# A graph attention layer on one core: the conversion of the adjacency matrix moved from GpSimd to VectorE

## The chip, the cores and the metric

The kernel runs on one core of a Trainium2 chip. The metric is the device time of one execution in microseconds (us). The core has five engines with a queue of instructions each: TensorE (PE in the profile, its weight loads as PEld), VectorE (DVE), ScalarE (ACT), GpSimd (POOL) and SyncE (SP). SP and POOL also issue DMA transfers here, and all transfers share 16 DMA engines.

## What is computed

The inputs are `x` (4096 x 256), a 0/1 matrix `adj` (4096 x 4096, float32, about 0.4% ones) and weights for 8 heads of key size 64.

```python
h = maximum(layernorm(x), 0)
adj = maximum(adj, eye)
q, k, v = h @ Wq, h @ Wk, h @ Wv                # per head
scores = q @ k.T * 64 ** -0.5
scores = scores + 0.01 * eye - 1e16 * (1 - adj)
att = softmax(scores)
return x + sum over heads of (att @ v) @ Wo
```

So every score gets a bias: 0 where `adj` is one or on the diagonal, a huge negative number elsewhere.

## The kernel before, in words

The 8 heads are worked on in two groups of 4 (`group_programs`, g = 0 and 1). A group first makes keys and values for all 4096 nodes (`keys_values`), then runs over 16 row blocks i of 256 rows (two tiles q = 0, 1 of 128 rows) and in each over its heads h = 0 to 3. One pair (i, h) is a step, 64 steps in a group. The order of every engine's work is written out by hand (`step` in each engine's program), and semaphores tie the engines together.

In step (i, h) TensorE transposes the probabilities of head h (`transposes`), multiplies them by the values (`values`, `values_late`), and between these computes the scores of the next head (`scores`, L449). The scores come in eight slots j of 128 x 1024, j = 0 to 3 for q = 0 and j = 4 to 7 for q = 1, into two PSUM buffers `psS`, so that the scores of slot j wait for the mask of slot j - 2. VectorE's `mask` (L702) adds the bias `B` to the slot, writes it to `S` and takes the row maximum. Per step VectorE runs masks 2 and 3 of the next head, `sum_halves` (L735, L740), masks 4 and 5, the denominators and sums of heads, masks 6 and 7, the transpose of half of the probabilities in 32 x 32 blocks for q = 0 (`transpose_late`, L723), masks 0 and 1 of the head after, and the transpose for q = 1. The blocks so transposed are put in their places by 32 DMA transfers per step, 64 KB each: 16 from SP (`move_late`, L248) and 16 from POOL (L307). The masks 4 to 7 write where these blocks are read from: masks 4 and 5 wait for the two halves of the moves of q = 0, masks 6 and 7 for those of q = 1. TensorE's last part of a step (`values_late`, L486) waits for all of them.

`B` (128 x 2 x 4096, bf16) holds the bias of one row block and serves all heads of it. In the first group POOL fills it: it loads eight slots of `adj` per row block with a cast to bf16 (`load_adj`, L287, 512 KB read and 256 KB written each), each as soon as the last head's mask has used the slot; it converts each slot in place (`convert`, L293: subtract 1, multiply by 8e16); and in the slot that holds the row block's own diagonal (`own_slot`, which moves from 0 to 3 over the row blocks) it multiplies 128 x 128 elements by `notI` (L298), which clears the bias on the diagonal. The loads and most converts stand in POOL's step h = 2, between and behind the moves of that step; the converts of slots (1, 2) and (1, 3) follow the moves of step h = 3. The masks of a row block's head 0 wait for `bias_ready`: masks 0 and 1 stand in VectorE's step h = 2, masks 2 to 7 in step h = 3. SP stores the finished bias in DRAM (`keep_bias`, in step h = 0), and the second group only loads it back, from SP's queue. Row block 0 is loaded and converted while keys and values are made.

The lines in question:

```python
B = sb("B", [P, QT, N], BF16)
mask: if h == 0 and norm: dve.wait_ge(bias_ready, i * SLOTS + (j + 1))
```

`norm` is true in the first group alone.

## Time and profile before

| | |
|---|---|
| three runs, us | 2713.36, 2710.54, 2719.93 (median 2713.36) |
| the profiled execution, us | 2709.6 |
| its span in the profile, us | 2708.1 |
| granted TensorE clock over the span | 0.994 of full speed |
| busy, share of the span | PE 97%, PEld 70%, DVE 83%, ACT 68%, POOL 47% |
| chain that ended last, by engine | PE 38%, SP's queue 3%, DVE 2%, DMA 2% |
| the first group's row blocks 0 to 14 | 118.8 to 1320.2 us |
| the second group's | 1473.1 to 2637.7 us |

The profile is one execution recorded by the hardware. Busy time is the share in which an engine had an instruction in work; an average hides what a single stretch is limited by. So stretches of the trace are looked at one by one, each with the times of its instructions and, in square brackets, the idle time ahead of an instruction and what ended it. A step is measured here from the first L486 matmul of one step to that of the next; the stretch that ends with the L486 matmuls of step (i, 2) is called step h = 2, and so on.

### The profile page before, as it was taken

The numbers are of one execution on the slowest core, as the hardware profiler recorded it, in microseconds if no ns is written. First come the engines' busy times: TensorE is split into PE (matmuls) and PEld (weight loads), VectorE is DVE, ScalarE is ACT, GpSimd is POOL, SyncE is SP. The second block draws the span as 40 slices with busy tenths as digits, with TensorE's granted clock in tenths as the row PEclk, the third lists the DMA queues.
The fourth block names the chain that finished last, engine by engine and source line by source line (L and its number), as shares of the span: only waits on it lengthen the run. The fifth ranks groups of instructions, "written<-read, shape, count | busy, mean of one in ns | idle before, by whom it ended". The sixth has DMA issues, their size and how long they took to land. (4 is left out here: it accounts for less than half of the span.)

```text
span 2708.1 us, 58752 instructions
## 1 busy us (share of the span) xinstructions
PE 2630.7 (97%) x17344; PEld 1901.9 (70%) x17344; DVE 2253.6 (83%) x3833; ACT 1850.8 (68%) x3041; POOL 1280.6 (47%) x2418
## 2 busy tenths in 40 slices
PE   7899999999999999999998999999999999999997
PEld 5666777767777776766766777777777777777775
DVE  6788888888888888888847888888888888888885
ACT  3576777767767676776745777777777777777774
POOL 2356655566565556655512444444444444343433
PEclk9999999999999999999999999999999999999999
DMA  6367766677776677776652566656565656555654
GB/s 163 111 143 177 184 163 175 165 168 167 173 190 170 164 177 166 171 171 169 167 142 76 146 158 151 158 142 145 138 151 145 164 146 162 133 146 138 157 144 106
DMA packets 263358, 418.51 MB, mean 155 GB/s; under 512 B 98944, under 2 KB 119936, under 8 KB 259200
## 3 DMA queue, kind: packets, MB, share of 16 engines
q1 hardware_dynamic: 172032, 228.88, 33.0%
q0 software_dynamic: 89088, 184.69, 29.7%
q10 hardware_dynamic: 2176, 4.19, 0.4%
q8 instruction: 28, 0.46, 0.1%
q14 instruction: 34, 0.28, 0.0%
HBM read 136.31 MB, written 46.27 MB: 67 GB/s over the span
## 5 line engine op out<-in xcount | busy, mean ns | idle before, releaser
L307 POOL DMA_DIRECT2D S<-S x2048 | 1007.8, 500 | 1137.1 <-DVE S L723 1089.6
L702 DVE CUSTOM_DVE_ANT_0 S<-psS,B 128x1024 f32<-128x1024 f32 x1024 | 1228.4, 1218 | 268.3 <-PE psS L449 155.1
L589 ACT ACTIVATE S<-S,negm 128x1024 f32<-128x1024 f32 (+1 forms) x768 | 1095.8, 1428 | 88.8 <-DVE negm L709 88.3
L596 ACT ACTIVATE PT<-psT 128x512 f32<-128x512 f32 x1024 | 595.0, 596 | 267.5 <-PE psT L462 248.5
L449 PE MATMUL psS<-K,QH 128*128 128x512 f32 x2048 | 729.2, 437 | 35.7 <-DVE mx L702 31.5
L449 PE MATMUL psS<-K,QL 128*128 128x512 f32 x2048 | 642.5, 395 | 0.0
L462 PEld LDWEIGHTS psT<-ident,S 128*128 128x128 f32 x4096 | 481.2, 140 | 192.0 <-issue 73.5
L462 PE MATMUL psT<-ident,S 128*128 128x128 f32 x4096 | 608.0, 276 | 7.8 <-ACT S L589 4.9
L723 DVE STREAM_TRANSPOSE S<-S 128x2048 f32<-128x2048 f32 x256 | 590.2, 2306 | 27.6 <-PE psO L486 23.7
L472 PE MATMUL psO<-PT,V 128*64 128x256 f32 x4096 | 492.1, 382 | 0.0
L486 PE MATMUL psO<-S,V 128*64 128x256 f32 x4096 | 470.3, 382 | 2.0 <-DMA S<-S 2.0
L449 PEld LDWEIGHTS psS<-K,QL 128*128 128x128 f32 x2048 | 385.3, 188 | 87.4
L486 PEld LDWEIGHTS psO<-S,V 128*64 128x64 f32 x4096 | 283.6, 137 | 176.5 <-issue 48.0
L472 PEld LDWEIGHTS psO<-PT,V 128*64 128x64 f32 x4096 | 283.4, 137 | 175.0 <-ACT PT L596 23.7
L449 PEld LDWEIGHTS psS<-K,QH 128*128 128x128 f32 x2048 | 313.6, 191 | 82.0 <-DVE mx L702 69.6
L623 ACT ACTIVATE Oodd<-psO 64x256 f32<-64x256 f32 x128 | 48.9, 382 | 400.7 <-PE psO L472 400.7
L293 POOL TENSOR_SCALAR B<-B 128x1024 bf16<-128x1024 bf16 x128 | 133.4, 1052 | 59.6 <-DMA B<-in_adj 58.4
L589 ACT ACTIVATION_READ_ACCUMULATOR S<-S,negm 128x1 f32 x768 | 146.0, 190 | 0.0
L685 DVE TENSOR_TENSOR QL<-psP,QH 64x256 fp32r<-64x256 f32 x248 | 104.4, 421 | 3.6
L708 DVE TENSOR_TENSOR S<-S,diag 128x128 f32 (+1 forms) x256 | 75.2, 294 | 30.9 <-DVE mx L702 23.3
L580 ACT ACTIVATE QH<-psP 64x256 fp32r<-64x256 f32 x248 | 93.1, 375 | 2.2
L702 DVE DVE_READ_ACCUMULATOR2_ANT mx<- 128x1 f32 x1024 | 84.9, 83 | 0.0
(51 smaller groups left out, 967.9 us busy)
## 6 DMA issues: line engine op xcount, KB each, us to landing
S<-S SPq DMA_DIRECT2D x2048, 64.0 KB, 3.1
S<-S POOLq DMA_DIRECT2D x2048, 64.0 KB, 2.9
B<-in_adj POOLq DMA_DIRECT2D x128, 256.0 KB, 7.2
bias_scratch<-B SPq DMA_DIRECT2D x32, 1024.0 KB, 5.8
B<-bias_scratch SPq DMA_DIRECT2D x128, 256.0 KB, 5.1
hq<-hT_scratch SPq DMA_DIRECT2D x32, 256.0 KB, 3.5
RB<-rden_scratch SPq DMA_DIRECT2D x128, 64.0 KB, 3.2
S<-in_x SPq DMA_DIRECT2D x8, 512.0 KB, 3.6
```

The lines of the kernel that those rows point to most:

```text
L293: done = nc.gpsimd.tensor_scalar(part, part, -1.0, MASK_VAL / SCALE, ALU.add, ALU.mult)
L307: pool.dma_start(dst, src).then_inc(late_sent[q][half], 16)
L449: last = nc.tensor.matmul(psS[j % 2][:, b * BANK:(b + 1) * BANK], part[:, h, q * P:(q + 1) * P], K2[:, h, col:col + BANK], start=hi, stop= ...
L462: last = nc.tensor.transpose(psT[s % 2][:, a * QW + q * P:a * QW + (q + 1) * P], S[:, h % 2, q, col:col + P], ident[:, :])
L472: last = nc.tensor.matmul(psO[a * KD:(a + 1) * KD, 0:QW], V[:, 2 * s + a, h * KD:(h + 1) * KD], PT[:, s % RING, a * QW:(a + 1) * QW], star ...
L486: last = nc.tensor.matmul(psO[half_ * KD:(half_ + 1) * KD, 0:QW], V[:, MT - LATE + m, h * KD:(h + 1) * KD], PTL[:, m, :, :, :], start=Fals ...
L580: last = nc.scalar.activation(QH[half_ * KD:(half_ + 1) * KD, h + e, :], query_psum(first)[e * KD:(e + 1) * KD, 0:QW], ACT.Copy)
L589: nc.scalar.activation(part, part, ACT.Exp, bias=negm[:, h % 2, q:q + 1], accum_out=sums[:, h % 2, q, e:e + 1]).then_inc(probs_ready, 1)
L596: nc.scalar.activation(PT[:, s % RING, :], psT[s % 2][:, :], ACT.Copy).then_inc(pt_act, 1)
L685: last = nc.vector.tensor_tensor(QL[rows, h + e, :], query_psum(first)[e * KD:(e + 1) * KD, 0:QW], QH.bitcast(F32)[rows, h + e, :], ALU.su ...
L702: nc.vector.tensor_tensor_reduce(out=part, in0=psS[j % 2][:, :], in1=B[:, q, k * SLOT:(k + 1) * SLOT], scale=SCALE, scalar=LOWEST, op0=ALU ...
L723: nc.vector.transpose(dst, src).then_inc(late_transposed, 1)
```

## The change

POOL no longer converts. VectorE converts each slot itself, right ahead of the mask of head 0 that uses it. POOL's part for the diagonal now works on the raw 0/1 values, ahead of the conversion: it multiplies the own block by `notI` and adds `eye`, a new 128 x 128 constant, so that the diagonal is one. VectorE's conversions wait for this (`self_added`) and for the slot's load (`adj_in`), and each mask waits for its conversion (`bias_ready`). POOL's order changes with it: the four loads of q = 0 stand behind both moves of step h = 2 (before, two of them stood between the moves), then the diagonal of q = 0, then the four loads of q = 1; the diagonal of q = 1 stands between the two moves of step h = 3.

```diff
-        def convert(i, q, k, own_slot):
-
-            wait_apart(pool, adj_in[q][k], i * 16 + 16, pool_passed)
-            part = B[:, q, k * SLOT:(k + 1) * SLOT]
-            done = nc.gpsimd.tensor_scalar(part, part, -1.0, MASK_VAL / SCALE, ALU.add, ALU.mult)
-            if k == own_slot:
-                done.then_inc(bias_conv, 1)
-                pool.wait_ge(bias_conv, i * QT + q + 1)
-                own = B[:, q, bass.ds(i * QW + q * P, P)]
-                done = nc.gpsimd.tensor_tensor(own, own, notI[:, :], ALU.mult)
-            done.then_inc(bias_ready, 1)
+        def add_self(i, q, own_slot):
+
+            wait_apart(pool, adj_in[q][own_slot], i * 16 + 16, pool_passed)
+            own = B[:, q, bass.ds(i * QW + q * P, P)]
+            nc.gpsimd.tensor_tensor(own, own, notI[:, :], ALU.mult).then_inc(self_cleared, 1)
+            wait_apart(pool, self_cleared, i * QT + (q + 1), pool_passed)
+            nc.gpsimd.tensor_tensor(own, own, eye[:, :], ALU.add).then_inc(self_added, 1)
...
             for q in range(QT):
-                for k in range(SPT):
-                    convert(0, q, k, 0)
+                add_self(0, q, 0)
...
             move_late(i, h, 0)
-            if adj_step:
-                for k in range(2):
-                    load_adj(i + 1, 0, k)
+            if adj_rest:
+                add_self(i + 1, 1, own_slot)
             move_late(i, h, 1)
-            if adj_step:
-                for k in range(2, SPT):
-                    load_adj(i + 1, 0, k)
             if prev and h == 1:
                 store(i - 1)
+            if adj_step:
+                for k in range(SPT):
+                    load_adj(i + 1, 0, k)
             if prev and h == 2:
                 pool.wait_ge(stored, i * 16)
                 load_base(i)
             if adj_step:
-                for half_ in range(2):
-                    for k in (2 * half_, 2 * half_ + 1):
-                        convert(i + 1, 0, k, own_slot)
-                    for k in (2 * half_, 2 * half_ + 1):
-                        load_adj(i + 1, 1, k)
-                for k in range(2):
-                    convert(i + 1, 1, k, own_slot)
-            if adj_rest:
-                for k in range(2, SPT):
-                    convert(i + 1, 1, k, own_slot)
+                add_self(i + 1, 0, own_slot)
+                for k in range(SPT):
+                    load_adj(i + 1, 1, k)
...
             if h == 0 and norm:
+                dve.wait_ge(self_added, i * QT + (q + 1))
+                wait_apart(dve, adj_in[q][k], i * 16 + 16, dve_passed)
+                part = B[:, q, k * SLOT:(k + 1) * SLOT]
+                nc.vector.tensor_scalar(part, part, -1.0, MASK_VAL / SCALE, ALU.add, ALU.mult).then_inc(bias_ready, 1)
                 dve.wait_ge(bias_ready, i * SLOTS + (j + 1))
```

Two places show what moves. The first is POOL's queue in step h = 2 of the first group, around the moves of the late blocks (`S<-S`). Before:

```order
L307 DMA S<-S 32x512 x8
L78 ISA
L285 REGISTER_ALU
L287 ISA
L287 DMA B<-in_adj 128x1024
L285 REGISTER_ALU
L287 ISA
L287 DMA B<-in_adj 128x1024
L78 REGISTER_ALU
L307 DMA S<-S 32x512 x8
```

With the change:

```order
L303 DMA S<-S 32x512 x8
L78 REGISTER_ALU
L303 DMA S<-S 32x512 x8
L78 ISA
L285 REGISTER_ALU
L287 ISA
L287 DMA B<-in_adj 128x1024
```

The moves of q = 1 (the second group of eight) no longer stand behind two loads; all four loads of q = 0 follow them.

The second is VectorE's queue in step h = 3, at masks 4 and 5 of the next row block's head 0 (an ISA row with `S,mx<-psS,B` is a mask). Before:

```order
L740 TENSOR_TENSOR O<-Oodd,RB 64x256
L693 REGISTER_ALU
L78 REGISTER_ALU
L702 ISA S,mx<-psS,B 128x1024
L702 ISA mx 128x1
L693 REGISTER_ALU
L78 REGISTER_ALU
L702 ISA S,mx<-psS,B 128x1024
L702 ISA mx 128x1
```

With the change:

```order
L732 TENSOR_TENSOR O<-Oodd,RB 64x256
L681 REGISTER_ALU
L684 TENSOR_SCALAR B<-B 128x1024
L685 REGISTER_ALU
L78 REGISTER_ALU
L694 ISA S,mx<-psS,B 128x1024
L694 ISA mx 128x1
L684 TENSOR_SCALAR B<-B 128x1024
L685 REGISTER_ALU
L78 REGISTER_ALU
L694 ISA S,mx<-psS,B 128x1024
L694 ISA mx 128x1
```

Every one of the eight masks of head 0 in a row block has a conversion of 128 x 1024 elements (L684) ahead of it now.

## Rows read from the trace of the kernel before

**Rows 1.** The page, busy time of each engine over the span.
```profile
PE 2630.7 (97%) x17344; PEld 1901.9 (70%) x17344; DVE 2253.6 (83%) x3833; ACT 1850.8 (68%) x3041; POOL 1280.6 (47%) x2418
```

**Rows 2.** Windows: 60 steps of each group; last columns clock, DMA share, GB/s.
```profile
118.80:1320.20 1201.40, 1177.29 (x7923) 850.97 (x7922) 1018.46 (x1710) 842.55 (x1381) 696.44 (x1258) 1.00 0.71 170
1473.10:2637.70 1164.60, 1161.78 (x7921) 850.52 (x7920) 1016.38 (x1710) 840.22 (x1381) 492.18 (x988) 1.00 0.61 148
```

**Rows 3.** Windows, first group: sum of the 15 h = 2 steps, then h = 3.
```profile
sum 322.76, PE 309.10 PEld 223.69 DVE 264.24 ACT 222.13 POOL 235.86; mean PE 20.61 PEld 14.91 DVE 17.62 ACT 14.81 POOL 15.72
...
sum 292.89, PE 285.73 PEld 201.31 DVE 246.38 ACT 199.26 POOL 213.92; mean PE 19.05 PEld 13.42 DVE 16.43 ACT 13.28 POOL 14.26
```

**Rows 4.** Windows, second group: sum of the 15 h = 2 steps, then h = 3.
```profile
sum 306.76, PE 305.07 PEld 223.51 DVE 264.73 ACT 222.67 POOL 128.31; mean PE 20.34 PEld 14.90 DVE 17.65 ACT 14.84 POOL 8.55
...
sum 279.23, PE 278.10 PEld 200.96 DVE 242.56 ACT 195.50 POOL 118.00; mean PE 18.54 PEld 13.40 DVE 16.17 ACT 13.03 POOL 7.87
```

**Rows 5.** Timeline of DVE, masks 6 and 7 in step h = 2 (start, length).
```profile
637.78 1.22 DVE L702 CUSTOM_DVE_ANT_0 S<-psS,B 128x1024 f32<-128x1024 f32 x1 [0.87 <-DMA S<-S]
...
640.45 1.23 DVE L702 CUSTOM_DVE_ANT_0 S<-psS,B 128x1024 f32<-128x1024 f32 x1 [1.44 <-PE psS L449]
```

**Rows 6.** Timeline of POOL: h = 2 loads and q = 1 moves; h = 3 moves.
```profile
627.57 1.21 POOL L287 DMA_DIRECT2D B<-in_adj  x2
628.90 3.96 POOL L307 DMA_DIRECT2D S<-S  x8
...
648.37 7.93 POOL L307 DMA_DIRECT2D S<-S  x16 [0.23 <-issue]
```

**Rows 7.** Timeline of SP's queue, the 16 moves of the same step h = 2.
```profile
623.07 10.93 SPq L248 DMA_DIRECT2D S<-S  x16
```

**Rows 8.** DMA issues, us to landing: in 628.8:631, 602.8:621.4 (step h = 1), 632.8:634.
```profile
S<-S SPq DMA_DIRECT2D x4, 64.0 KB, 6.6
...
S<-S SPq DMA_DIRECT2D x16, 64.0 KB, 4.3
...
B<-in_adj POOLq DMA_DIRECT2D x2, 256.0 KB, 8.2
```

**Rows 9.** Timeline of DVE, masks 2 to 7 of a second-group step h = 3.
```profile
1790.79 1.23 DVE L702 CUSTOM_DVE_ANT_0 S<-psS,B 128x1024 f32<-128x1024 f32 x1 [1.00 <-PE psS L449]
...
1792.16 1.23 DVE L702 CUSTOM_DVE_ANT_0 S<-psS,B 128x1024 f32<-128x1024 f32 x1
...
1794.66 1.22 DVE L702 CUSTOM_DVE_ANT_0 S<-psS,B 128x1024 f32<-128x1024 f32 x1
...
1795.81 1.22 DVE L702 CUSTOM_DVE_ANT_0 S<-psS,B 128x1024 f32<-128x1024 f32 x1
...
1798.27 1.22 DVE L702 CUSTOM_DVE_ANT_0 S<-psS,B 128x1024 f32<-128x1024 f32 x1 [0.21 <-PE psS L449]
...
1799.62 1.23 DVE L702 CUSTOM_DVE_ANT_0 S<-psS,B 128x1024 f32<-128x1024 f32 x1
```

**Rows 10.** L658 by line (duration ns min/median/max), and L708 in the timeline.
```profile
L658 DVE TENSOR_SCALAR S<-S,mv,rstd x32: 395/406/1126, 8.1 to 70.8; 128x256 f32<-128x256 f32 x32
...
601.15 0.29 DVE L708 TENSOR_TENSOR S<-S,diag 128x128 f32 x1 [0.15 <-DVE mx L702]
```

**Rows 11.** Timeline of DVE and POOL: L658 beside DMA issues, and beside tensor operations.
```profile
12.66 1.39 DVE L658 TENSOR_SCALAR S<-S,mv,rstd 128x256 f32<-128x256 f32 x4 [1.13 <-POOL rstd L319]
...
12.59 4.49 POOL L287 DMA_DIRECT2D B<-in_adj  x8
...
68.32 3.62 DVE L658 TENSOR_SCALAR S<-S,mv,rstd 128x256 f32<-128x256 f32 x4
...
68.62 4.21 POOL L293 TENSOR_SCALAR B<-B 128x1024 bf16<-128x1024 bf16 x4
```

**Rows 12.** Timeline of DVE, masks 4 and 6 of row block 0, head 0.
```profile
92.36 1.21 DVE L702 CUSTOM_DVE_ANT_0 S<-psS,B 128x1024 f32<-128x1024 f32 x1
...
95.02 1.22 DVE L702 CUSTOM_DVE_ANT_0 S<-psS,B 128x1024 f32<-128x1024 f32 x1 [0.29 <-issue]
```

More of the change, by code:

```diff
@@ L82, in group_programs @@
 def group_programs(nc, sem, g, before, x, hT, adj, bias, Wk, Wq, Wv, Wo, base, result, t):
-    (K2, V, S, B, PT, QH, QL, hq, wq, wo, O, Oodd, RB, acc, res, ident, notI, diag, mx, negm, sums, den, rden,
+    (K2, V, S, B, PT, QH, QL, hq, wq, wo, O, Oodd, RB, acc, res, ident, notI, eye, diag, mx, negm, sums, den, rden,
      stats, mv, rstd, half, xb, hc, wk, wv, psS, psT, psO, psP, rden_scratch, ones_set, consts) = t
@@ L111, in group_programs @@
     bias_kept = sem(f"bias_kept{g}")
-    (bias_conv, bias_ready, q_proj, q_hi, q_lo, scores_ready, slot_masked, row_ready, probs_ready,
+    (self_cleared, self_added, bias_ready, q_proj, q_hi, q_lo, scores_ready, slot_masked, row_ready, probs_ready,
      transposed, pt_act, pt_free, o_ready, projected, summed, den_ready, head_added,
@@ L115, in group_programs @@
         sem(f"{s}{g}") for s in (
-            "bias_conv", "bias_ready", "q_proj", "q_hi", "q_lo", "scores_ready", "slot_masked", "row_ready",
+            "self_cleared", "self_added", "bias_ready", "q_proj", "q_hi", "q_lo", "scores_ready", "slot_masked", "row_ready",
             "probs_ready", "transposed", "pt_act", "pt_free", "o_ready", "projected", "summed", "den_ready",
@@ L324, in constants @@
             nc.gpsimd.memset(notI[:, :], 1.0).then_inc(ones_set, 1)
+            nc.gpsimd.memset(eye[:, :], 0.0).then_inc(ones_set, 1)
             nc.gpsimd.memset(diag[:, :], 0.0).then_inc(ones_set, 1)
-            pool.wait_ge(ones_set, 3)
-            for m, fill in ((ident, 1.0), (notI, 0.0), (diag, IDENTITY_BIAS)):
+            pool.wait_ge(ones_set, 4)
+            for m, fill in ((ident, 1.0), (notI, 0.0), (eye, 1.0), (diag, IDENTITY_BIAS)):
                 nc.gpsimd.affine_select(out=m[:, :], in_=m[:, :], compare_op=ALU.not_equal, fill=fill, base=0,
                                         pattern=[[-1, P]], channel_multiplier=1).then_inc(consts, 1)
-            pool.wait_ge(consts, 3)
+            pool.wait_ge(consts, 4)
         if norm:
@@ L531, in tensor_program @@
         if norm:
-            pe.wait_ge(consts, 3)
+            pe.wait_ge(consts, 4)
             transpose_x(0, 0)
@@ L797, in vector_program @@
         if norm:
-            dve.wait_ge(consts, 3)
+            dve.wait_ge(consts, 4)
             for b in range(2):
@@ L843, in build @@
         notI = sb("notI", [P, P], BF16)
+        eye = sb("eye", [P, P], BF16)
         diag = sb("diag", [P, P])
@@ L865, in build @@
         ones_set, consts = sem("ones_set"), sem("consts")
-        tiles = (K2, V, S, B, PT, QH, QL, hq, wq, wo, O, Oodd, RB, acc, res, ident, notI, diag, mx, negm, sums, den, rden,
+        tiles = (K2, V, S, B, PT, QH, QL, hq, wq, wo, O, Oodd, RB, acc, res, ident, notI, eye, diag, mx, negm, sums, den, rden,
                  stats, mv, rstd, half, xb, hc, wk, wv, psS, psT, psO, psP, rden_scratch, ones_set, consts)
```

## The prediction

> **What bounds the kernel now.** I read the page first: TensorE is busy for 97% of the span and VectorE for 83% [rows 1], so TensorE sets the pace and VectorE has little room. The two groups do the same arithmetic per step and differ in how the bias reaches `B`: in the first POOL loads and converts it, in the second SP loads it ready made. So the second group is a yardstick inside the same trace. Over the 60 steps of row blocks 0 to 14 the first group takes 1201.4 us and the second 1164.6 [rows 2]: everything that the adjacency costs in this stretch is 36.8 us, 1.4% of the time, and no rearrangement of it can win much more.
>
> Then I cut the stretch into kinds of step. The 15 steps h = 2 take 322.8 us in the first group, 21.5 each [rows 3], and 306.8, 20.45 each, in the second [rows 4]. The 15 steps h = 3 take 292.9, 19.5 each [rows 3], against 279.2, 18.6 each [rows 4]. That is 16.0 and 13.7 of the 36.8 us; the other 7.1 lie in the two kinds of step in which the change moves nothing.
>
> Why h = 2 is slow shows in VectorE's timeline. Mask 6 begins after 0.87 us of waiting for a move (`DMA S<-S`), and mask 7 begins 2.67 us after it where 1.15 would do [rows 5]. The second wait is put down to TensorE, whose scores had long been done; the moves of q = 1, second half, are the other thing mask 7 waits for. POOL issued two loads of adjacency at 627.57 and only then the moves of q = 1, to 632.86 [rows 6]; SP issued its 16 moves until 634.00 [rows 7]. In this traffic SP's moves take 6.6 us to land, in step h = 1 4.3 us [rows 8]: 634.0 + 6.6 = 640.6 is just where mask 7 starts. So it is SP's last moves, slowed by the loads in the shared DMA engines, that hold mask 7, and POOL's late queue holds mask 6. In h = 3 POOL begins its moves at 648.37, all 16 in a row, because it was still converting [rows 6].
>
> **The change, part by part.**
>
> *Step h = 2, masks 6 and 7.* POOL's moves of q = 1 pass two loads, whose issue took 1.2 us [rows 6], so they go out 1.3 us earlier and into an emptier queue: mask 6's wait of 0.87 goes. What is late next is mask 7, held by SP's last moves at 634.0. The loads now begin at about 627.57 + 3.96 = 631.5, when POOL's moves are issued, and come four in a row, so SP's last three or four moves still meet them. SP's backlog by then is smaller: I take a landing of 5.5 us, between 4.3 and 6.6 [rows 8], which brings mask 7 forward by 1.1 us. Bounds: with 6.6 us nothing is gained; at the other end the step falls to the second group's 20.45 and a little below, a gain of 1.3. I take 0.9 us per row block, for a step of 20.6: **-13.5 us** over 15.
>
> *Step h = 3, five conversions on the path.* VectorE is what TensorE waits for here, since scores wait for the mask two slots before. Masks 2 to 7 of an undisturbed step start at 1790.79, 1792.16, 1794.66, 1795.81, 1798.27 and 1799.62 [rows 9]. A mask behind another without any wait comes after 1.15 us (the pair 4, 5). So the slack of VectorE in this stretch is 1.37 - 1.15 = 0.22 ahead of mask 3, 0.21 idle ahead of mask 6 and 1.35 - 1.15 = 0.20 ahead of mask 7, together 0.63 us. The conversion for mask 2 is free: VectorE sits idle for 1.00 us there [rows 9]. The five for masks 3 to 7 stand in line.
>
> The trace has no such conversion on VectorE. The nearest row by operation is the `tensor_scalar` on SBUF data at L658, 0.41 us for 256 float32 elements [rows 10]; by number of elements it is the mask, 1.22 us for 1024 [rows 9]. I take the first, since the elements here are half as wide and the operation is the same. To it comes the wait of the mask for its end: 0.15 us lies between a mask and the operation that waits for it [rows 10]. So a conversion costs 0.41 + 0.15 = 0.56, with bounds of 0.41 and 1.37.
>
> Then 5 x 0.56 - 0.63 = 2.2 us over an undisturbed step, 18.6 + 2.2 = 20.8, against 19.5 now: +1.3 per row block, **+19.5 us**. The 0.9 us that h = 3 loses now to late moves does not come on top: POOL's moves of q = 0 go out as soon as VectorE has transposed, with no conversions ahead of them as there were at 648.37, and masks 4 and 5 come later.
>
> *Step h = 2, the conversions for masks 0 and 1.* 1.1 us ahead of the transpose for q = 1. TensorE has `values_late` and four `values` to do before it needs these masks, so nothing is lost by them; the transpose comes later by up to 1.1, and the 1.00 us of idle time behind it covers that or nearly so. Without that cover they would cost up to 0.7 us more in h = 3; it goes into the range.
>
> *The own slot.* Masks now wait for the diagonal, and the diagonal for its slot's load. For slot 0, issued first, that is early. For slot 3 (the blocks 12 to 15, so four of them) the load is issued last, at about 631.5 + 2 x 1.21 = 633.9, lands after 8.2 us [rows 8] at 642.1, and POOL's two operations follow. In that case POOL's four loads of q = 1 go out after 643, its moves of h = 3 behind them, and the diagonal of q = 1 waits again for a load, with the moves of q = 1 behind it. I charge 1.5 us for each of the four, between 0 and 4: **+6 us**.
>
> *Row block 0.* Two masks take 95.02 - 92.36 = 2.66 us [rows 12]. With conversions two take 2 x (1.15 + 0.56) = 3.42, so 0.76 more, four times: **+3 us**. POOL's eight conversions there lay beside keys and values and cost nothing; nor do they now.
>
> *GpSimd's removed conversions* are worth nothing by themselves: POOL is busy for 47% [rows 1]. What they delay is counted above.
>
> Sum: -13.5 + 19.5 + 6 + 3 = +15 us on the profiled execution's 2709.6, so **2724.6**, say 2725. The median of the three runs, 2713.4, is 3.8 above that execution; from there it would be 2728, inside the range.
>
> **The rivals.**
>
> *Relief outweighs the conversions (faster).* The place is mask 7 of step h = 2. If SP's last moves land as in step h = 1, after 4.3 us [rows 8], the step falls by 1.3 us: -19.5. If a conversion also costs no more than 0.44, h = 3 goes to 18.6 + 2.2 - 0.63 = 20.2, +0.65 per block: +10. With +1 for row block 0 and nothing for the own slot the sum is -8.5: 2701. It decides as soon as h = 2 gains more than h = 3 loses. For it: POOL's queue is freed of 8 conversions per block, and DMA traffic is spread later. Against it: four loads in one go fall exactly on SP's last moves. Chance 0.15.
>
> *Both effects cancel.* Gain of 1.2 and loss of 0.9 us per block, own slot and block 0 at +5: 2710 to 2716. Chance 0.15.
>
> *The conversion is dearer.* Near the middle of the bounds, 0.85 with its wait: 5 x 0.85 - 0.63 = 3.6, h = 3 at 22.2, +2.7 x 15 = +40, block 0 +5, own slot +6, less 13.5: +38, 2748. Chance 0.12. At the upper bound of 1.37: 6.2 in h = 3, a step of 24.8, +80, and block 0 +10: +82, 2792. Chance 0.03.
>
> *The port.* Four L658 took 1.39 us beside POOL's DMA issues, and 3.62 us beside POOL's tensor operations [rows 11]. So an operation of this kind on VectorE and a tensor operation on POOL do shut each other out, and a DMA issue on POOL does not: its eight went at 0.56 each in that stretch. POOL's tensor work beside the new conversions is only the diagonal, 4 short operations per block, which I leave in the range. SBUF — State Buffer in the Trainium skill (SBUF: two separate sides) says more: a two-port operation on VectorE also keeps GpSimd from writing its DMA descriptors; by this rule conversions and POOL's moves would stand in each other's way. The rows of this trace speak against it. If each of the five conversions lost 0.25 us, half of a move's issue of 0.5 [rows 6], that would be 1.25 per block, +19 more: 2744. Chance 0.05.
>
> **The numbers.** My forecast holds 0.50, with a range of its own of 2714 to 2736. A measurement of this kernel tells a change of 0.3%, 8 us, from none, so same means about 2705 to 2721.5. Of the forecast 0.40 lies above, 0.10 inside. Slower: 0.40 + 0.12 + 0.03 + 0.05 = 0.60. Same: 0.10 + 0.15 = 0.25. Faster: 0.15. The range of 2702 to 2750 takes in the cancelling case, most of the faster one, the port and the half-way price, and leaves out the ends.
>
> **What would show it.** In the new profile: conversions on VectorE of 0.4 us, each mask some 0.55 later; steps h = 3 at 20.8 us with masks 3 to 7 waiting for nothing but VectorE itself; steps h = 2 at 20.6 with mask 6 no longer waiting for a move and mask 7 still waiting a little; the last four blocks a little worse than the first; the second group unchanged. The prediction is wrong if h = 3 does not grow by more than h = 2 shrinks, or if a conversion takes over 0.6 us.

## The result, and the profile after

The changed kernel takes 2753.8 us in the median of four runs (2751.6 to 2755.1) against 2715.4 (2710.5 to 2719.9) for the kernel before beside it: a ratio of 1.014, 95% interval 1.0126 to 1.0154. That is 38 us slower where 15 were forecast, and 3.8 us above the top of the range. The sign was right, the size was not.

The page, in the line that answers to [rows 1], shows TensorE's share down by a point, VectorE 46 us busier and POOL 121 us less busy:

```profile
PE 2643.3 (96%) x17344; PEld 1904.7 (69%) x17344; DVE 2299.4 (84%) x3961; ACT 1853.8 (67%) x3041; POOL 1160.0 (42%) x2324
```

The two stretches of 60 steps, as [rows 2] (columns: span, busy us of PE, PEld, DVE, ACT and POOL, granted clock, DMA share, GB/s):

```profile
122.45:1359.95 1237.50, 1185.64 (x7921) 852.93 (x7920) 1060.78 (x1830) 845.32 (x1381) 584.79 (x1168) 1.00 0.69 165
1514.69:2683.29 1168.60, 1164.84 (x7921) 850.28 (x7920) 1017.84 (x1710) 840.38 (x1381) 490.57 (x988) 1.00 0.60 148
```

The first group's stretch grew from 1201.4 to 1237.5 us and begins 3.6 us later; the second group, which the change does not touch, differs by 4 us from one execution to the other. The sums over the 15 steps h = 2 and the 15 steps h = 3 of the first group, as [rows 3]:

```profile
sum 302.86, PE 302.49 PEld 224.21 DVE 273.21 ACT 229.78 POOL 180.20; mean PE 20.17 PEld 14.95 DVE 18.21 ACT 15.32 POOL 12.01
...
sum 343.46, PE 298.36 PEld 202.53 DVE 280.76 ACT 194.40 POOL 159.46; mean PE 19.89 PEld 13.50 DVE 18.72 ACT 12.96 POOL 10.63
```

Here is the whole story in two numbers. Steps h = 2 went from 21.5 to 20.2 us each, 19.9 us won. Steps h = 3 went from 19.5 to 22.9, 50.6 us lost. The rest of the 45.5 us between the two spans is small: 3.6 ahead of row block 0, 5.5 in the steps h = 1 and h = 0 (where the steps h = 1 are between 18.9 and 19.5 us in the mean in all fourteen kernels of the table below), 1.8 between the two stretches and 4 in the second group.

Step h = 2, which answers to [rows 5], now has masks 6 and 7 without any wait for a move, 1.19 us apart (mask 7 still waits 1.0 to 1.4 us in row blocks 0, 1 and 4, and less than 0.5 elsewhere). With TensorE busy for 20.17 of the 20.19 us, such a step has nothing left to win:

```profile
648.76 1.22 DVE L694 CUSTOM_DVE_ANT_0 S<-psS,B 128x1024 f32<-128x1024 f32 x1 [0.18 <-issue]
...
649.95 1.22 DVE L694 CUSTOM_DVE_ANT_0 S<-psS,B 128x1024 f32<-128x1024 f32 x1
```

And the step h = 3 behind it, VectorE's timeline from mask 2 to mask 7 (L694 is a mask, L684 a conversion), to be read against [rows 9]; the step begins at 653.27:

```profile
660.38 1.23 DVE L694 CUSTOM_DVE_ANT_0 S<-psS,B 128x1024 f32<-128x1024 f32 x1 [0.31 <-PE psS L437]
...
661.53 0.42 DVE L684 TENSOR_SCALAR B<-B 128x1024 bf16<-128x1024 bf16 x1
662.23 1.23 DVE L694 CUSTOM_DVE_ANT_0 S<-psS,B 128x1024 f32<-128x1024 f32 x1 [0.27 <-DVE B L684]
...
664.67 0.41 DVE L684 TENSOR_SCALAR B<-B 128x1024 bf16<-128x1024 bf16 x1
666.61 1.23 DVE L694 CUSTOM_DVE_ANT_0 S<-psS,B 128x1024 f32<-128x1024 f32 x1 [1.52 <-DMA S<-S]
...
671.60 1.23 DVE L694 CUSTOM_DVE_ANT_0 S<-psS,B 128x1024 f32<-128x1024 f32 x1 [0.28 <-DVE B L684]
...
673.45 1.23 DVE L694 CUSTOM_DVE_ANT_0 S<-psS,B 128x1024 f32<-128x1024 f32 x1 [0.28 <-DVE B L684]
```

Two things are to be seen. A conversion takes 0.42 us as forecast, but the mask that waits for it starts 0.28 us after its end and not 0.15, so that each one costs 0.70 us in line (661.53 to 662.23). And mask 4 waits 1.52 us for a late move, the wait that the prediction had said would not come on top. The transfers issued in the first 8.7 us of that step, with their time to landing (first row the loads of q = 1), say why:

```profile
B<-in_adj POOLq DMA_DIRECT2D x3, 256.0 KB, 7.9
S<-S POOLq DMA_DIRECT2D x9, 64.0 KB, 8.3
S<-S SPq DMA_DIRECT2D x7, 64.0 KB, 6.7
RB<-rden_scratch SPq DMA_DIRECT2D x1, 64.0 KB, 6.7
```

POOL's timeline has the four loads of q = 1 in one go just ahead of its moves:

```profile
652.23 2.53 POOL L287 DMA_DIRECT2D B<-in_adj  x4 [0.25 <-issue]
654.74 3.96 POOL L303 DMA_DIRECT2D S<-S  x8
```

In the kernel before, the four were issued two and two around POOL's conversions, in the same row block 5.1 us ahead of the step's start (642.87) and 0.9 us behind it, and the moves of that step only from 648.37 on [rows 6]:

```profile
637.76 1.18 POOL L287 DMA_DIRECT2D B<-in_adj  x2 [0.24 <-issue]
...
643.78 1.10 POOL L287 DMA_DIRECT2D B<-in_adj  x2
```

So the change moved two of these loads 4.1 us later and the other two 0.6 us earlier, and POOL's first moves 4.0 us earlier, from 5.5 to 1.5 us behind the step's start: now loads and moves go out together. In this traffic moves of 64 KB take 6.7 to 8.3 us. SP's queue adds to it: it stood still until the 1 KB store of the denominators had landed, 7.9 us after its issue, and began its moves only after 657.

```profile
648.61 0.34 SPq L264 DMA_DIRECT2D rden_scratch<-rden  x1
656.49 0.48 SPq L267 DMA_DIRECT2D RB<-rden_scratch  x1
657.07 10.87 SPq L248 DMA_DIRECT2D S<-S  x16
```

The last four steps h = 3, whose next row block has own slot 3, are longer for one more reason: 23.3 to 26.4 us, against 22.35 in the mean of the first eleven. In the longest, POOL waits 5.77 us for the load that it issued last, then does the diagonal, and VectorE's conversion for mask 4 waits 2.47 us for that:

```profile
1157.39 0.42 POOL L293 TENSOR_TENSOR B<-B,notI 128x128 bf16 x1 [5.77 <-DMA B<-in_adj]
...
1158.60 0.43 DVE L684 TENSOR_SCALAR B<-B 128x1024 bf16<-128x1024 bf16 x1 [2.47 <-POOL B L295]
```

In the first eleven no conversion waits for POOL. These two kinds of row block have to be kept apart below, since a mean over all fifteen mixes them.

So, the own slot aside, there were three candidates for the 3.4 us that h = 3 lost: VectorE's line of conversions, the traffic of the loads, and SP's late start. My theory after the result was that the first two are two limits that run side by side.

### The profile page after: what moved, and what is told of

It is laid out like the page before. It is cut to its first block, busy times and chain, and to the rows that moved or that the text cites. A ratio compares the mean times of both kernels' runs of the same rounds, so it can differ in the third digit from the quotient of the medians.

```text
span 2753.6 us, 58893 instructions
## 1 busy us (share of the span) xinstructions
PE 2643.3 (96%) x17344; PEld 1904.7 (69%) x17344; DVE 2299.4 (84%) x3961; ACT 1853.8 (67%) x3041; POOL 1160.0 (42%) x2324
## 4 chain that ended last, share of the span: by engine, by line
PE 62%; DMA 13%; DVE 7%; SPq 7%; issue 7%; POOL 2%; DVEq 0%; ACT 0%; POOLq 0%; ACTq 0%
PE psS L437 23%; PE psO L474 12%; PE psT L450 11%; PE psO L460 10%; SPq L248 6%; DMA S<-S 6%; DMA rden_scratch<-rden 4%; DMA B<-in_adj 4%; DVE S L694 3%; PE psS L395 2%; POOL S L303 2%; PE psP L422 2%; DVE S L715 1%; PE psP L484 1%; DVE QL L673 1%
## 5 line engine op out<-in xcount | busy, mean ns | idle before, releaser
L694 DVE CUSTOM_DVE_ANT_0 S<-psS,B 128x1024 f32<-128x1024 f32 x1024 | 1231.8, 1219 | 256.0 <-PE psS L437 130.9
L715 DVE STREAM_TRANSPOSE S<-S 128x2048 f32<-128x2048 f32 x256 | 590.2, 2306 | 27.2 <-PE psO L474 24.8
L700 DVE TENSOR_TENSOR S<-S,diag 128x128 f32 (+1 forms) x256 | 75.2, 294 | 29.0 <-DVE mx L694 21.4
L694 DVE DVE_READ_ACCUMULATOR2_ANT mx<- 128x1 f32 x1024 | 85.2, 83 | 0.0
L554 ACT ACTIVATE K<-psS 64x512 f32 (+1 forms) x64 | 37.9, 593 | 57.9 <-PE psS L395 57.1
```

The lines of the kernel that those rows point to most:

```text
L694: nc.vector.tensor_tensor_reduce(out=part, in0=psS[j % 2][:, :], in1=B[:, q, k * SLOT:(k + 1) * SLOT], scale=SCALE, scalar=LOWEST, op0=ALU ...
L715: nc.vector.transpose(dst, src).then_inc(late_transposed, 1)
```

## The experiments

Times are medians; the ratio is to the kernel before, run on the same chip beside it (its median was between 2705 and 2727 us from one set to the next, so ratios are what can be compared). The last columns are the mean us of a step in each execution that was profiled, over row blocks 0 to 14 of the first group. They come from one execution each: e10's was the fastest of its six, 11 us below the median, and e11's the slowest, 9 us above it, which is worth up to 0.7 us in the sum of the two columns.

| kernel | us | ratio (95%) | h = 2 | h = 3 |
|---|---|---|---|---|
| before | 2715.4 | 1 | 21.52 | 19.53 |
| the change | 2753.8 | 1.0140 (1.0126 to 1.0154) | 20.19 | 22.90 |
| e1 two loads between the moves | 2764.3 | 1.0151 (1.0123 to 1.0178) | 21.40 | 22.11 |
| e2 before, order of the change | 2744.7 | 1.0070 (1.0046 to 1.0093) | 20.38 | 22.00 |
| e3 conversion one mask ahead | 2748.2 | 1.0093 (1.0065 to 1.0120) | 20.21 | 22.29 |
| e4 denominators' load later | 2758.0 | 1.0126 (1.0100 to 1.0151) | 20.24 | 22.64 |
| e5 light loads of q = 1 | 2729.4 | 1.0082 (1.0059 to 1.0106) | 20.18 | 21.81 |
| e6 light loads, conversion ahead | 2682.4 | 0.9913 (0.9889 to 0.9936) | 20.15 | 19.07 |
| e7 diagonal behind the moves | 2746.2 | 1.0151 (1.0127 to 1.0176) | 20.17 | 22.94 |
| e8 before, two conversions later | 2718.8 | 1.0046 (1.0029 to 1.0064) | 21.43 | 20.20 |
| e9 e1 and e3 together | 2721.0 | 1.0054 (1.0039 to 1.0069) | 21.36 | 20.40 |
| e10 one load between, ahead | 2721.2 | 1.0052 (1.0039 to 1.0065) | 20.15 | 21.04 |
| e11 before, one load between | 2717.5 | 1.0046 (1.0029 to 1.0063) | 20.72 | 21.05 |
| e12 e10, own slot first | 2715.5 | 1.0035 (1.0022 to 1.0049) | 20.45 | 20.93 |

**e1, two loads back between the moves.**

```diff
@@ step of GpSimd, changed kernel
+            if adj_step:
+                for k in range(2):
+                    load_adj(i + 1, 0, k)
             move_late(i, h, 1)
...
-                for k in range(SPT):
+                for k in range(2, SPT):
                     load_adj(i + 1, 0, k)
```

Expected: 

> The changed kernel with two of the four loads of q = 0 put back between POOL's moves of step h = 2. Theory: the order of the loads alone made steps h = 2 short (20.2 us each), and the conversions with the late moves made steps h = 3 long (22.9). Then h = 2 goes back to about 21.5, h = 3 stays at 22.9, and the time is about 2754 + 20 = 2774. Rival: POOL's queue, free of conversions, is what shortened h = 2; then the time stays at 2754 to 2758.

Steps h = 2 went back to 21.4, as the theory had it, so it is the place of the loads and not POOL's missing conversions that made them short. The ratio rose only to 1.0151, because h = 3 fell by 0.8 to 22.1. VectorE's masks 2 to 7 in such a step show no wait for a move at all; everything is the line of conversions, from a mask 2 that is 0.8 us late (668.90 is 7.9 us after the step's start; undisturbed it is 7.1). Masks 2, 3, 4 and 7:

```profile
668.90 1.22 DVE L697 CUSTOM_DVE_ANT_0 S<-psS,B 128x1024 f32<-128x1024 f32 x1 [0.27 <-DVE B L687]
670.75 1.22 DVE L697 CUSTOM_DVE_ANT_0 S<-psS,B 128x1024 f32<-128x1024 f32 x1 [0.27 <-DVE B L687]
673.88 1.22 DVE L697 CUSTOM_DVE_ANT_0 S<-psS,B 128x1024 f32<-128x1024 f32 x1 [0.28 <-DVE B L687]
...
680.53 1.22 DVE L697 CUSTOM_DVE_ANT_0 S<-psS,B 128x1024 f32<-128x1024 f32 x1 [0.28 <-DVE B L687]
```

So VectorE alone is enough for 22 us where mask 2 is late.

**e2, the kernel before with the order of the change.** POOL still converts.

```diff
@@ step of GpSimd, kernel before
-            if adj_step:
+            if adj_rest:
                 for k in range(2):
-                    load_adj(i + 1, 0, k)
+                    convert(i + 1, 1, k, own_slot)
             move_late(i, h, 1)
-            if adj_step:
-                for k in range(2, SPT):
-                    load_adj(i + 1, 0, k)
             if prev and h == 1:
                 store(i - 1)
+            if adj_step:
+                for k in range(SPT):
+                    load_adj(i + 1, 0, k)
...
-                for k in range(2):
-                    convert(i + 1, 1, k, own_slot)
             if adj_rest:
                 for k in range(2, SPT):
                     convert(i + 1, 1, k, own_slot)
```

Expected: 

> The kernel before with the load order of the change alone: POOL still converts, all loads of q = 0 behind both moves of step h = 2, and the first two conversions of q = 1 between the moves of h = 3. Theory: h = 2 falls to 20.2 (-20 us over 15 row blocks); in h = 3 POOL's moves of q = 0 start no earlier than before and in heavier traffic, but VectorE has no conversions, so masks 4 and 5 wait and the step is 19.5 to 20.5 (0 to +15). The time is 2695 to 2710. Rival: what makes h = 3 long in the changed kernel is the traffic of four loads of q = 1 in a row and not VectorE; then h = 3 is over 21.5 here too and the time is 2725 or more.

The kernel is 0.7% slower than the one before where the theory had it faster, and the rival was right in its numbers: with no conversion on VectorE the steps h = 3 are 22.0 us all the same. The moves of such a step take some 6.2 us to land (mean over the first eleven of the median of a step; 3.5 for POOL's and 4.1 for SP's in the kernel before), and masks 4 and 5, and often mask 7, wait for them. The gain of 1.1 us in h = 2 is paid back with 2.5. Not all of the 2.5 is the order of the loads: the two conversions between the moves were put there too, and by themselves they cost 0.7 (e8).

**e3, each conversion one mask ahead.**

```diff
@@ mask of VectorE, changed kernel; convert(i, j) is its waits and the tensor_scalar of slot j
             if h == 0 and norm:
-                dve.wait_ge(self_added, i * QT + (q + 1))
-                wait_apart(dve, adj_in[q][k], i * 16 + 16, dve_passed)
-                part = B[:, q, k * SLOT:(k + 1) * SLOT]
-                nc.vector.tensor_scalar(part, part, -1.0, MASK_VAL / SCALE, ALU.add, ALU.mult).then_inc(bias_ready, 1)
+                if j == 0:
+                    convert(i, 0)
+                if j + 1 < SLOTS and j != 3:
+                    convert(i, j + 1)
                 dve.wait_ge(bias_ready, i * SLOTS + (j + 1))
...
+            if h == 0 and norm and j == 3:
+                convert(i, 4)
```

Expected: 

> The changed kernel with each conversion one mask earlier, so that no mask waits for the conversion just ahead of it. Theory: a conversion costs 0.70 us in line (0.42 and a wait of 0.28) and 0.35 without the wait. If a late move holds mask 4 in step h = 3, only the conversions behind it count, three times 0.35: -16 us, 2738. If nothing but VectorE holds it, five times 0.35: -26 us, 2728. Rival: the 0.28 us is the drain of any VectorE instruction and not the wait for its end; then the time stays within 4 us of 2754.

The ratio went from 1.0140 to 1.0093, some 13 us, and h = 3 from 22.9 to 22.3 in the mean: less than the 16 us of the case in which a move holds mask 4. The first eleven row blocks gain 1.0 us each, from 22.35 to 21.4, but the last four lose 0.3, from 24.4 to 24.75: the conversion for mask 4 now stands ahead of other work on VectorE and waits there 3.7 to 4.4 us for the diagonal. The conversions did get cheaper, as the rows of masks 5 and 6 show: 0.34 us in line (660.34 to 660.68) instead of 0.70. But mask 4 waits for a move as before:

```profile
656.51 1.22 DVE L702 CUSTOM_DVE_ANT_0 S<-psS,B 128x1024 f32<-128x1024 f32 x1 [1.55 <-DMA S<-S]
657.66 0.42 DVE L683 TENSOR_SCALAR B<-B 128x1024 bf16<-128x1024 bf16 x1
658.10 1.22 DVE L702 CUSTOM_DVE_ANT_0 S<-psS,B 128x1024 f32<-128x1024 f32 x1
660.34 0.42 DVE L683 TENSOR_SCALAR B<-B 128x1024 bf16<-128x1024 bf16 x1
660.68 1.21 DVE L702 CUSTOM_DVE_ANT_0 S<-psS,B 128x1024 f32<-128x1024 f32 x1
```

**e4, SP's load of the denominators behind the first four moves of h = 3.**

```diff
@@ SyncE, changed kernel; load_rden is the two waits and the load of RB
                     sp.dma_start(dst, src).then_inc(late_moved[q][half], 16)
+                if norm and h == 3 and q == 0 and half == 0:
+                    load_rden(i, 2)
...
-            sp.wait_ge(rden_stored, count(i, h, 16, 16 + 16 * START))
-            sp.wait_ge(o_ready, count(i, h, 1, START))
-            sp.dma_start(RB[:, :], ...).then_inc(rden_in, 16)
+            if not (norm and h == 2):
+                load_rden(i, h)
```

Expected: 

> The changed kernel with SP's load of the reciprocal denominators (RB) of step h = 2 moved behind the first four moves of step h = 3. In the changed kernel SP stands still at that load until the 1 KB store ahead of it has landed (7.9 us), so its moves of h = 3 begin 2.3 us later than before, and mask 4 waits 1.5 us for them. Theory A: this late start is the cause; the wait at mask 4 goes, h = 3 falls by 1.2 to 1.5 us, the time to about 2734. Theory B: the moves land late because four loads of q = 1 share the DMA engines with them, whenever SP issues them; then the gain is 0 to 5 us.

Theory A falls: h = 3 is 22.6, within 0.3 of the change. SP's moves now begin 0.5 to 0.8 us into the step in twelve of the fifteen (1.5 in the others), and where mask 4 no longer waits for them, the wait has gone to the denominators, which land 7.0 us after their issue in the step shown. VectorE's timeline of it (L738 multiplies by them, and its wait is put down to "issue"):

```profile
664.84 0.41 DVE L733 TENSOR_TENSOR Oodd<-psO,Oodd 64x256 f32<-64x256 f32 x1
666.92 0.42 DVE L738 TENSOR_TENSOR O<-Oodd,RB 64x256 f32<-64x256 f32 x1 [1.68 <-issue]
667.30 0.43 DVE L690 TENSOR_SCALAR B<-B 128x1024 bf16<-128x1024 bf16 x1
```

Whatever SP issues in this stretch lands late; the order in SP's queue only chooses what.

**e5 and e6, light loads.** Both cut the loads of q = 1 to an eighth, and their conversions for q = 1 add 0 and multiply by 1, so these two kernels leave the adjacency of q = 1 out; e6 also has e3's edit.

```diff
-            rows = adj[bass.ds(i * QW + q * P, P), k * SLOT:(k + 1) * SLOT]
-            pool.dma_start(B[:, q, k * SLOT:(k + 1) * SLOT], rows).then_inc(adj_in[q][k], 16)
+            width = SLOT if first or q == 0 else P
+            rows = adj[bass.ds(i * QW + q * P, P), k * SLOT:k * SLOT + width]
+            pool.dma_start(B[:, q, k * SLOT:k * SLOT + width], rows).then_inc(adj_in[q][k], 16)
```

Expected of e5: 

> The changed kernel with the loads of q = 1 cut from 1024 to 128 columns each; its conversions run over as many elements as before, but those of q = 1 add 0 and multiply by 1, so the adjacency of q = 1 is left out of the computation. Theory: two limits overlap in steps h = 3, VectorE's line of conversions (five times 0.70 us less 0.63 of slack: 18.4 + 2.9 = 21.3, up to 22.0 with masks 0 to 2 late) and moves and denominators that land late in the traffic of the loads of q = 1. Without that traffic only the first is left: h = 3 at 21.3 to 22.0 against 22.9 in the changed kernel, 13 to 24 us less, and no mask of h = 3 waits for a move. Rival 1, VectorE alone is the 22.9: less than 5 us. Rival 2, the traffic is nearly all of it: h = 3 under 20.5, over 36 us less.

Expected of e6: 

> The same cut loads of q = 1 together with each conversion one mask ahead (as in e3). If both limits are real, taking both away gives more than the sum of what each gave alone: h = 3 at 18.4 + 5 x 0.35 - 0.6 = 19.6 against 22.9 in the changed kernel and 22.3 in e3, so about 50 us less than the changed kernel and at or below the kernel before. Rival, the limits do not overlap: e5's gain plus e3's 0.6 us per step, that is h = 3 near 21.

With e3 these make a square, in us of a step h = 3:

| | conversion just ahead of its mask | one mask ahead |
|---|---|---|
| full loads | 22.90 | 22.29 (-0.61) |
| light loads | 21.81 (-1.09) | 19.07 (-3.83) |

Each alone gives little, both together more than twice their sum. But light loads land sooner too, and so do the diagonals behind them, so part of this is the own slot. The first eleven row blocks, in which nothing waited for a diagonal in the change, show the two limits by themselves:

| first eleven | conversion just ahead of its mask | one mask ahead |
|---|---|---|
| full loads | 22.35 | 21.39 (-0.96) |
| light loads | 21.55 (-0.80) | 18.95 (-3.40) |

Both together still give almost twice the sum. That is the mark of two limits side by side, where the step takes the longer of the two. In e5 the moves issued in the first 8.6 us of a step h = 3 land after 2.6 us (POOL's) and 2.8 us (SP's), against 8.3 and 6.7 with full loads; over whole steps, first eleven, it is 3.1 and 3.2 against 6.5 and 6.0:

```profile
S<-S POOLq DMA_DIRECT2D x11, 64.0 KB, 2.6
S<-S SPq DMA_DIRECT2D x9, 64.0 KB, 2.8
```

and no mask of the steps h = 3 waits for one. In this step mask 2 starts 7.1 us behind the step's start, as in an undisturbed one, and masks 4 and 7 are held by their conversions alone:

```profile
653.52 1.22 DVE L695 CUSTOM_DVE_ANT_0 S<-psS,B 128x1024 f32<-128x1024 f32 x1 [0.27 <-PE psS L438]
...
658.50 1.22 DVE L695 CUSTOM_DVE_ANT_0 S<-psS,B 128x1024 f32<-128x1024 f32 x1 [0.28 <-DVE B L685]
...
665.14 1.23 DVE L695 CUSTOM_DVE_ANT_0 S<-psS,B 128x1024 f32<-128x1024 f32 x1 [0.28 <-DVE B L685]
```

So a step of 21.55 us, as in the first eleven, is what VectorE's line costs; the 21.8 of all fifteen has some waiting for the diagonal in it (0.5 to 1.3 us in each of the last four). In e6, with neither limit, masks 4 to 7 run without a wait, a conversion costing 0.34 us, and the step is 0.5 us shorter than even the 19.6 I had written down:

```profile
639.00 1.21 DVE L703 CUSTOM_DVE_ANT_0 S<-psS,B 128x1024 f32<-128x1024 f32 x1
640.14 0.41 DVE L684 TENSOR_SCALAR B<-B 128x1024 bf16<-128x1024 bf16 x1
640.48 1.21 DVE L703 CUSTOM_DVE_ANT_0 S<-psS,B 128x1024 f32<-128x1024 f32 x1
...
644.19 1.22 DVE L703 CUSTOM_DVE_ANT_0 S<-psS,B 128x1024 f32<-128x1024 f32 x1
```

**e7, the diagonal of q = 1 behind both moves of h = 3.** `add_self(i + 1, 1, own_slot)` stands behind `move_late(i, h, 1)` and not ahead of it.

Expected: 

> The changed kernel with the diagonal of q = 1 behind both of POOL's moves of step h = 3 instead of between them. In the changed kernel the four row blocks whose own slot is 3 have steps h = 3 of 23.8, 26.4, 24.1 and 23.3 us against 22.4 for the others. Theory: POOL waits there for the last load with the moves of q = 1 behind it; without that these four fall by 1 to 2 us each, 4 to 8 us in all, and the others do not change. Rival: the diagonal of q = 0 behind the last of its loads is the cause; then they stay as they are, or get worse because mask 4 now waits for the diagonal of q = 1.

The four steps h = 3 with own slot 3 are 23.0, 23.3, 23.4 and 24.8 us, together 3.2 less than in the change, and the first eleven are 22.7 instead of 22.35 in the mean; the mean of all is 22.94 and the ratio unchanged within its interval. In the four, POOL's wait for the last load was moved and not removed: VectorE's conversion for mask 4 still stands behind it, for 0.5 to 1.5 us. In the others that conversion, which waited for nothing, now waits about 1.07 us in nine of the eleven for a diagonal that stands behind 16 moves. The theory had them unchanged.

**e8, the kernel before with POOL's first two conversions of q = 1 between its moves of h = 3.**

```diff
+            if adj_rest:
+                for k in range(2):
+                    convert(i + 1, 1, k, own_slot)
             move_late(i, h, 1)
...
-                for k in range(2):
-                    convert(i + 1, 1, k, own_slot)
             if adj_rest:
                 for k in range(2, SPT):
```

Expected: 

> The kernel before with one thing moved: POOL's first two conversions of q = 1 stand between its moves of step h = 3 and not ahead of them. Before, POOL begins these moves 4 us after VectorE has transposed, and masks 4 and 5 wait 0.4 to 1.4 us. If POOL's lateness is what they wait for, h = 3 falls from 19.5 to about 18.8 and the time by 8 to 12 us (0.3 to 0.45%). If SP's moves, slowed by the loads, are what they wait for, the time stays within 3 us.

It is 0.46% slower, which neither case allowed for: h = 3 grew by 0.7. POOL's moves of q = 0 begin 2.9 us earlier (first eleven, mean), but now they go out close behind the loads and beside more of SP's moves: POOL's take 5.6 us to land instead of 3.5 and SP's 5.7 instead of 4.1. POOL's last of q = 0 lands only 0.4 us earlier and the last of q = 1 lands 1.6 us later, so that masks 6 and 7, which waited for nothing before, have a wait of 0.4 to 0.9 us in most steps. This is in small what the change did: POOL's conversions had kept its moves out of the traffic.

**e9, e10 and e12, versions that might beat the kernel before.** e9 is e1 and e3 together. e10 is e9 with one load of q = 0 between the moves of h = 2 in place of two. e12 is e10 with

```diff
-                for k in range(1, SPT):
+                for k in sorted(range(1, SPT), key=lambda k: k != own_slot):
                     load_adj(i + 1, 0, k)
...
-                for k in range(SPT):
+                for k in sorted(range(SPT), key=lambda k: k != own_slot):
                     load_adj(i + 1, 1, k)
```

Expected of e9: 

> e1 and e3 together: two loads of q = 0 between POOL's moves of h = 2, and each conversion one mask ahead. In e1 no mask of the steps h = 3 read out waited for a move (VectorE alone made them 22.0), so here, unlike in e3, the conversion ahead should pay in full. Theory (two overlapping limits): h = 2 stays at 21.4, h = 3 falls from 22.1 by five times 0.35 and by most of the late start of mask 2 to 19.3 to 20.3; together 40.7 to 41.7 against 41.05 in the kernel before and 43.1 in the changed one: 0.995 to 1.005 of the kernel before. Rival (the conversion ahead is worth 0.6 us whatever the loads do, as in e3): h = 3 at 21.5 and a ratio of about 1.011.

Expected of e10: 

> As e9, with only one load of q = 0 between the moves of h = 2 and three behind them. If the loads between the moves cost h = 2 in proportion, h = 2 is at 20.7 to 20.9; the loads of q = 1 then come about where they do in e3, so h = 3 has part of the traffic back: 20 to 21. The sum is within 0.5 us of e9's and the ratio within 0.4% of it. If instead a single load ahead of the moves already delays SP's last ones, h = 2 is 21.4 as in e9 and this is the slower of the two by 0.3% or more.

Expected of e12: 

> e10 with the own slot loaded first among those of q = 1, and first of the three of q = 0 that follow the moves. In e10 the steps h = 3 are 20.1 us in the median of row blocks with own slot 0 and 1 and 23.1 for own slot 3. Theory: VectorE and POOL's moves wait for the diagonal, and the diagonal for the load that is issued last. Then the rows with own slot 3 fall to 20 to 21 and the mean of h = 3 from 21.0 to about 20.2 (-12 us): 0.999 to 1.002 of the kernel before. Rival: the own slot's place is not the reason (later row blocks are slower for another one); then the time stays as e10's.

e9 came out just above its band at 1.0054. Its steps h = 3 are 18.8 to 19.5 us in the first seven row blocks and 21.4 to 22.9 in the last four. In the last four VectorE waits 2.4 to 3.0 us for the diagonal, whose slot is loaded last there; the four in between, 20.5 to 21.1, wait for moves. e10 is the same as e9 within the intervals, with h = 2 at 20.15: one load between the moves cost h = 2 nothing in the mean there (in e11 and e12 it is 0.3 to 0.6 us above e10's, by a few long steps), two cost 1.2. e12 brought the last four from 23.1 to 21.7 in the median, but the first seven rose from 20.1 to 20.7, the mean fell by 0.1 only, and the intervals of the ratios, 1.0022 to 1.0049 and 1.0039 to 1.0065, overlap. In the last four no conversion waits for a diagonal any more, but mask 4 waits 1.6 to 1.9 us for a move instead. That the own slot's wait is part of it is shown, that loading it first pays is not. None of the three beats the kernel before.

**e11, the kernel before with one load of q = 0 between the moves and three behind.**

Expected: 

> The kernel before with one load of q = 0 between POOL's moves of step h = 2 instead of two; POOL still converts, in its old order. In e10 one load between them left h = 2 at 20.15, so here too h = 2 should fall from 21.5 to 20.2 (-20 us). The loads run about 1 us later, and h = 3, which waits for late moves already, grows from 19.5: by less than 0.7 (time 0.993 to 0.997 of the kernel before) if only the sum of the traffic matters, by 1.3 or more (time the same or slower) if h = 2 and h = 3 only hand the same delay to each other.

h = 2 fell by 0.8 and h = 3 grew by 1.5; the ratio is 1.0046. This is the second of the two cases: the two steps hand the delay of the loads to each other. Here it goes less by slow moves (3.8 us to landing for POOL's against 3.5, first eleven) than by POOL's queue: its conversions wait for the later loads, and its moves of h = 3 begin 6.7 us into the step instead of 5.3; mask 4 waits 1.2 to 3.7 us for a move in thirteen of the fifteen. With e2 and e8 it makes three kernels in which VectorE converts nothing and traffic or conversions moved later on POOL alone cost 12 to 19 us.

## Why the prediction was wrong

- **Step h = 3: +19.5 us and the own slot's +6 forecast, +50.6 measured.** This is where it failed, and first of all in one sentence: that the late moves' share "does not come on top". It compared only when POOL issues its moves, and not what shares the DMA engines with them. POOL's first moves do go out earlier, 2.0 us into the step instead of 5.3 (first eleven, mean), but the last of these eight lands later, 13.7 us into it instead of 13.0, since now all four loads of q = 1 are in flight beside them; SP's, which also start late, at 2.9 instead of 1.5, land at 14.6 instead of 10.8. Put at nothing, it measured 22.35 against 21.55 us, 0.8 us per block (e5 against the change), about 12 us over 15. The rows for it were there: loads landing after 8.2 us and moves after 6.6 [rows 8], with the four loads to be issued in one go right at the start of the step.
- **In the same step, the price of a conversion in line.** The wait for its end is 0.28 us, not the 0.15 of the mask and its follower [rows 10]; five times 0.14 more makes 0.7 us per block. It was inside the bounds (0.70 against 0.41 to 1.37). The two conversions ahead of the transpose for q = 1 were put at nothing with "up to 0.7" left to the range; in e5 mask 2 is up to 0.8 us late, 0.3 in the mean of the first eleven, in e1 0.8. Undisturbed 18.4 + 5 x 0.70 - 0.63 = 21.3, with the 0.3 it is 21.6, and 21.55 was measured without traffic. That is about 30 us over 15 where 19.5 were forecast. With the 12 of the traffic and the 8 of the own slot it makes up the 50.6; the split is an estimate, since it takes the first eleven row blocks for all.
- **The own slot: +6 us forecast.** The four blocks cost 23.8, 26.4, 24.1 and 23.3 us against 22.35 for the others in the mean, together 8.3 more. Right within the bounds, and by the wait that it named.
- **Step h = 2, masks 6 and 7: -13.5 us forecast, -19.9 measured.** Right in mechanism, and e1 shows that it is the place of the loads. The landing of 5.5 us was a good choice: the slowest of SP's last four moves takes 5.4 us in the mean of the 15 steps (6.9 before). What the sum left out is that SP's queue runs sooner too; its last move is issued 11.2 us into the step and not 11.9. So mask 7 mostly waits for nothing, the step is TensorE's own 20.1, and the bound for the gain, 1.3 us per block, was the value.
- **Row block 0: +3 us forecast, 3.6 measured.** Right.
- **A conversion takes 0.4 us: right,** 0.42 in the median, but with luck. The reason given, elements half as wide and the same operation, compares 1024 of 2 bytes with the 256 of 4 bytes of L658: twice the bytes and four times the elements, for the same time, and no row of the kernel before showed that. VectorE: DVE Perf Modes in the Trainium skill (the perf-mode tier table) puts a bf16 `tensor_scalar` from SBUF to SBUF in the 4x mode, four elements per cycle. The trace is in line with that, since 1024 elements take 0.42 us here where the mask takes 1.22.
- **The port: it is there, and too small to matter.** POOL's eight moves from 654.74 on, with a conversion at 655.55 beside them, took 3.96 us, as those of [rows 6] did without any. But some moves were held. In the first group's 60 steps ten of POOL's 960 moves took 0.62 to 0.78 us to issue, where the median is 0.50 and none took over 0.58 in the kernel before, and each of the ten ends 0.10 us behind the end of a conversion that began inside it:

```profile
826.63 0.78 POOL L303 DMA_DIRECT2D S<-S  x1
826.90 0.41 DVE L684 TENSOR_SCALAR B<-B 128x1024 bf16<-128x1024 bf16 x1
```

So the lock on descriptor writing that SBUF — State Buffer in the Trainium skill describes (SBUF: two separate sides) is seen here after all, against the prediction's reading that the rows speak against it. It costs POOL at most 0.28 us a time, some 2 us over the ten, on an engine that is busy for 42%.
- **The rivals.** "Relief outweighs the conversions" had its condition met, -19.9 us in h = 2, and lost all the same, because the relief was a loan from h = 3. "The conversion is dearer" came near in time (2748) for another reason: the conversion with its wait was 0.70 and not 0.85. The rival that was missing is this one: a transfer moved out of one step's way falls into the next one's. Nor did either of the two signs that the prediction named for being wrong show up; h = 3 grew by more than h = 2 shrank, and a conversion took less than 0.6 us. They tested the direction and the unit price, and not the term that was left out.

What stays open: which part of the 7.1 us that the two untouched kinds of step lose to the adjacency has to do with its loads, and whether any order of the eight loads beats that of the kernel before. Those tried here, with and without POOL's conversions, did not.

## What to carry to other kernels

Where loads and moves together keep the DMA engines full for a stretch (POOL's queue alone took 93.7% of them from 654 to 657 us in the change), a load moved later did not lose its cost here, it handed it to whatever was issued next; look at what lands in the following step before booking a gain in this one. An earlier issue is not an earlier landing: in the change and in e8 moves went out sooner, into traffic, and gained little or lost. When two limits run side by side, an experiment that lifts one shows almost nothing: lift both before calling either harmless, and look at kinds of row block apart where one kind has a wait of its own. And a conversion right ahead of its reader on the same engine costs its wait as well as its work; one instruction earlier, it cost half (0.34 us against 0.70).

## What the runs showed of the hardware that was not expected

- On VectorE a mask that waits for the 0.42 us conversion just ahead of it starts 0.70 us after the conversion's start; when another instruction stands between them, the conversion adds 0.34 us (e3, e6).
- A store of 1 KB took 7.9 us to land beside the loads of adjacency, where the median over the run is 3.2 us, and moves of 64 KB took 6.7 to 8.3 us beside full loads and 2.6 to 2.8 beside light ones (e5). Neither the small size nor SP's queue protected a transfer from POOL's loads here.
- A move whose issue on POOL is under way when a bf16 conversion starts on VectorE is held until 0.10 us behind the conversion's end: 0.62 to 0.78 us instead of 0.50 (ten moves in the change; 22 over 0.6 us in e1, up to 0.91 us in e3).
